# The opening of an attention and mixture-of-experts kernel: order of loads, roots, bias split and transposes

## The reference

```
xn = (x - mean(x)) / sqrt(var(x) + 1e-5)                # each row
q, k, v = xn @ wq.T + bq, xn @ wk.T + bk, xn @ wv.T + bv
off = 6 tanh(pw_w @ gelu(conv3(q) + dw_b) + pw_b)       # 16 heads x 12 samples a row
pos = clip(row + anchor + off, 0, 4095)                 # sampled by linear interpolation
attn = softmax(q . k[pos] / 4 - rel_scale |pos - row|)
s = (sum of attn * v[pos]) @ wo.T + bo
scores = xn @ Wr.T + br                                 # 8 experts; the best 2 of scores + biases_N
y = sum over these 2 of weight * ((silu(xn @ W1a + ..) * (xn @ W1b + ..)) @ W2 + bl2)
out = x + s * silu(y)
```

## Time and profile before

| | |
|---|---|
| runs | 1416.57, 1421.54, 1422.76 us |
| profiled execution | 1412.04 us, span from first to last instruction 1410.3 us |
| busy, share of the span | PE 94%, PEld 75%, DVE 88%, ACT 57%, POOL 53% |
| mean granted TensorE clock | 0.978 |
| DMA | 297.77 MB, mean 211 GB/s |

### The profile page before, as it was taken

How to read it: one execution, slowest core, us unless ns; L and a number is a source line. 1 busy time by engine, 2 the same in 40 slices (tenths; PEclk the granted TensorE clock), 3 DMA queues, 4 the chain that set the end, 5 groups by cost and what they waited for, 6 DMA issues and landing times. The chain is left out here.

```text
span 1410.3 us, 36326 instructions
## 1 busy us (share of the span) xinstructions
PE 1319.4 (94%) x13885; PEld 1057.6 (75%) x13885; DVE 1245.6 (88%) x1759; ACT 797.9 (57%) x1920; POOL 740.8 (53%) x441
## 2 busy tenths in 40 slices
PE   5998899897899999989999999999999978899987
PEld 4864566556788888868888888888888857777765
DVE  7856998987999999978999999999999999898971
ACT  2546788677545465435554454555465536676654
POOL 1000022101787887888886888886887862211031
PEclk9999999998999999999999999999999989999998
DMA  7952657856857777586777585877777469989679
GB/s 233 348 196 85 185 168 240 295 189 204 258 141 231 205 248 206 136 243 169 227 211 203 141 270 148 243 193 216 214 197 226 121 173 279 291 222 267 199 206 219
DMA packets 206905, 297.77 MB, mean 211 GB/s; under 512 B 21809, under 2 KB 164533, under 8 KB 206515
## 3 DMA queue, kind: packets, MB, share of 16 engines
q0 software_dynamic: 59968, 141.95, 38.3%
q1 hardware_dynamic: 119171, 141.43, 31.2%
q10 hardware_dynamic: 27632, 12.64, 3.5%
HBM read 186.30 MB, written 118.03 MB: 216 GB/s over the span
## 5 line engine op out<-in xcount | busy, mean ns | idle before, releaser
L1666 POOL DMA_INDIRECT moe_rows<-expert_mem,token_of x135 | 340.8, 2524 | 104.4 <-issue 69.7
L1633 POOL DMA_INDIRECT expert_mem<-xn_rows,token_of x131 | 250.0, 1908 | 54.4 <-issue 36.6
L1956 PE MATMUL pY<-expert_mem 128*128 x1080 | 253.2, 386 | 0.0
L1956 PEld LDWEIGHTS pY<-expert_mem 128*128 128x128 f32 x1080 | 199.0, 190 | 39.4 <-issue 13.6
L2154 DVE SCALAR_TENSOR_TENSOR mid<-pos_pair,mid 128x768 f32<-128x768 f32 x224 | 197.4, 952 | 0.5
L1800 ACT ACTIVATE expert_mem<-pA,b1sel 128x256 f32<-128x256 f32 (+1 forms) x300 | 110.1, 455 | 132.1 <-PE pA L1950 129.2
L1950 PE MATMUL pA<-mid,expert_mem 128*128 128x256 f32 (+1 forms) x816 | 171.0, 364 | 13.9 <-ACT mid L1772 6.8
L1950 PEld LDWEIGHTS pA<-mid,expert_mem 128*128 128x128 f32 x816 | 145.1, 194 | 33.8 <-issue 9.0
L262 DVE SCALAR_TENSOR_TENSOR mid<-mid 128x768 f32<-128x768 f32 x192 | 169.4, 951 | 0.0
L1950 PE MATMUL pB<-mid,expert_mem 128*128 128x256 f32 (+1 forms) x816 | 166.1, 357 | 0.0
L1811 ACT ACTIVATE expert_mem<-pB,b1sel 128x256 f32<-128x256 f32 (+1 forms) x300 | 110.7, 468 | 95.2 <-PE pB L1950 95.2
(11 more groups left out here) (282 smaller groups left out, 2409.0 us busy)
## 6 DMA issues: line engine op xcount, KB each, us to landing
expert_mem<-in_w_l POOLq DMA_DIRECT2D x51, 1024.0 KB, 7.7
bandT<-in_w_l POOLq DMA_DIRECT2D x24, 1024.0 KB, 7.5
band<-band_rows SPq DMA_DIRECT2D x256, 96.0 KB, 4.8
S_rows<-expert_mem SPq DMA_DIRECT2D x64, 376.0 KB, 4.0
band_rows<-wgt SPq DMA_DIRECT2D x12, 1536.0 KB, 9.2
pos_pair<-pos_rows SPq DMA_DIRECT2D x28, 384.0 KB, 5.8
xn_rows<-expert_mem SPq DMA_DIRECT2D x16, 512.0 KB, 5.4
v_rows<-expert_mem SPq DMA_DIRECT2D x16, 512.0 KB, 4.3
```

The source lines that it names most:

```text
L1633: nc.gpsimd.indirect_dma_start(out=xs[:, u, s], out_offset=None, in_=dram["xn"], in_offset=bass.IndirectOffsetOnAxis(ap=keep["inv"][:, 2 * ...
L1666: nc.gpsimd.indirect_dma_start(out=dram["moe"], out_offset=bass.IndirectOffsetOnAxis(ap=keep["inv"][:, 2 * n + s:2 * n + s + 1], axis=0), ...
L1956: mm = nc.tensor.matmul(pY[:, s], hid[:, h, c, s * P:(s + 1) * P], w2[:, c, ds(e * D, D)], start=False, stop=(closes and c == HC - 1))
```

## The change

On ScalarE the four small loads go; its order of roots and evacuations in the first steps is new. GpSimd issues the four small loads, behind its stores of zeros, counted on a semaphore of their own (`small_in`), which ScalarE and VectorE await behind the stage of rows. `wvr` gets its own semaphore too (`wvr_loaded`), awaited in front of values(0); TensorE's wait for the other weights goes in front of the projection. VectorE does its memsets first, then moments and normalise of steps 0, 1 and 2 in turn, then goes on as before, one step of moments ahead; the bias split goes behind the stage, in front of routing. TensorE transposes the identity 44 times into PSUM `pOff`, which isn't in use then, before transposes(0), and does values(0) before transposes(1).

```diff
--- before.py
+++ after.py
@@ -81,6 +81,7 @@
 PLACES_AT, EXPERTS_AT, MERGE_AT, TOKENS_AT = 7, 8, 13, 14
 OPEN_AT = 5
 ROWS_AHEAD = 4
+WAKE = 44
 BAND_SLOTS = 4
 MOE_SLOTS = 8
 W1_SLOTS = 3
@@ -403,6 +404,8 @@
         pRuns = pOff[:].rearrange("p u (b r) -> p u b r", r=P)
         pToken = pQK[:, 0, 0:HIGH]
 
+        wvr_loaded = sem("wvr_loaded")
+        small_in = sem("small_in")
         weights_in = sem("weights_in")
         bias_loaded = sem("bias_loaded")
         bias_zeroed = sem("bias_zeroed")
@@ -474,7 +477,7 @@
 
         TAIL = VROWS - TOKENS - REACH
         HALVES = SUBS // 2
-        WEIGHTS = 16 * 7
+        WEIGHTS = 16 * 2
         ROUTE_WEIGHTS = WEIGHTS + 16 * 5
         CONSTS = 8
 
@@ -633,6 +636,11 @@
             pool.dma_start(dram["xn"][TOKENS:, 0:D].rearrange("(s p) c -> p s c", p=P), zeros[:, None, :].broadcast_to([P, 2, D])).then_inc(pads_set, 16)
             pool.dma_start(dram["xn"][TOKENS:, D:].rearrange("(s p) c -> p s c", p=P),
                            zeros[:, None, 0:EXPERTS].broadcast_to([P, 2, EXPERTS])).then_inc(pads_set, 16)
+            pool.dma_start(keep["rel"][:], io["rel_scale"].partition_broadcast(P)).then_inc(small_in, 16)
+            pool.dma_start(keep["b1"][:], io["b_l1T"].rearrange("e p c -> p e c")).then_inc(small_in, 16)
+            pool.dma_start(br_bc[:], io["b_r"].partition_broadcast(P)).then_inc(small_in, 16)
+            pool.dma_start(bqk_col[:], io["b_qk"].rearrange("(k p) -> p k", p=P),
+                          allow_slow_non_contiguous=True).then_inc(small_in, 16)
             pool.wait_ge(gates_ready, 1)
             for q in range(4):
                 some = slice(q * TILES // 4, (q + 1) * TILES // 4)
@@ -676,14 +684,9 @@
 
         @block.scalar
         def _(act):
-            act.dma_start(wvr[:], io["w_vrT"].rearrange("(k p) n -> p k n", p=P)).then_inc(weights_in, 16)
+            act.dma_start(wvr[:], io["w_vrT"].rearrange("(k p) n -> p k n", p=P)).then_inc(wvr_loaded, 16)
             act.dma_start(wqk[:, :, 0:D], io["w_qkT"].rearrange("(k p) n -> p k n", p=P)[:, :, 0:D]).then_inc(weights_in, 16)
             act.dma_start(wqk[:, :, D:], io["w_qkT"].rearrange("(k p) n -> p k n", p=P)[:, :, D:]).then_inc(weights_in, 16)
-            act.dma_start(keep["rel"][:], io["rel_scale"].partition_broadcast(P)).then_inc(weights_in, 16)
-            act.dma_start(keep["b1"][:], io["b_l1T"].rearrange("e p c -> p e c")).then_inc(weights_in, 16)
-            act.dma_start(br_bc[:], io["b_r"].partition_broadcast(P)).then_inc(weights_in, 16)
-            act.dma_start(bqk_col[:], io["b_qk"].rearrange("(k p) -> p k", p=P),
-                          allow_slow_non_contiguous=True).then_inc(weights_in, 16)
 
             def root(n):
                 act.wait_ge(var_ready, n + 1)
@@ -780,7 +783,13 @@
             root(0)
             root(1)
             evacuate_x(0)
-            for n in range(STEPS):
+            root(2)
+            evacuate_v(0)
+            evacuate_x(1)
+            evacuate_x(2)
+            root(3)
+            evacuate_v(1)
+            for n in range(2, STEPS):
                 if n + 2 < STEPS:
                     root(n + 2)
                 if n + 1 < STEPS:
@@ -788,6 +797,7 @@
                 evacuate_v(n)
 
             act.wait_ge(weights_in, ROUTE_WEIGHTS)
+            act.wait_ge(small_in, 16 * 4)
             act.wait_ge(mask_set, 1)
             for m in range(2):
                 evacuate_k(m)
@@ -960,17 +970,21 @@
                 nc.tensor.matmul(pToken, pieces[0:LINEAR - P, 1, 0], goes_to[0:LINEAR - P, 1], start=False, stop=True).then_inc(token_done, 1)
 
             pe.wait_ge(zeros_set, 3)
+            for _ in range(WAKE):
+                nc.tensor.transpose(pOff[:, 0, 0:P], keep["ident"][:], keep["ident"][:])
             transposes(0)
-            pe.wait_ge(weights_in, WEIGHTS)
-            for n in range(STEPS):
+            pe.wait_ge(wvr_loaded, 16)
+            values(0)
+            transposes(1)
+            for n in range(1, STEPS):
                 if n + 1 < STEPS:
                     transposes(n + 1)
                 values(n)
 
+            pe.wait_ge(weights_in, ROUTE_WEIGHTS)
             for m in range(2):
                 project(m, 0)
                 project(m, 1)
-            pe.wait_ge(weights_in, ROUTE_WEIGHTS)
             for n in range(STEPS):
                 more = n + 2 < STEPS
                 head_scores(n, 0)
@@ -1307,7 +1321,6 @@
                     dve.sem_inc(keep["scored"], 1)
 
             V.memset(bias_in[:, D:], 0.0).then_inc(bias_zeroed, 1)
-            moments(0)
             for b in range(BATCH):
                 for col in (b * (SEQ + 2), b * (SEQ + 2) + SEQ + 1):
                     V.memset(qT[:, :, col:col + 1], 0.0)
@@ -1316,17 +1329,11 @@
             for x in range(SAMPLES):
                 V.memset(anchor[:, x], anchors()[sample_at(x)])
             V.memset(zero_te[:], 0.0)
-            moments(1)
-            normalise(0)
-            moments(2)
-            normalise(1)
-            dve.wait_ge(bias_loaded, 32)
-            parts = Chain(dve, bias_chain)
-            for k in range(NB):
-                parts(V.tensor_copy(bias_part[:, k], bias_in))
-                if k < NB - 1:
-                    parts(V.tensor_tensor(bias_in, bias_in, bias_part[:, k], ALU.subtract))
-            for n in range(2, STEPS):
+            for n in range(3):
+                moments(n)
+                normalise(n)
+            moments(3)
+            for n in range(3, STEPS):
                 if n + 1 < STEPS:
                     moments(n + 1)
                 normalise(n)
@@ -1352,10 +1359,17 @@
             chain(V.tensor_tensor(to_row[:, 0:1], to_row[:, 0:1], to_row[:, 1:2], ALU.add))
             chain(V.tensor_copy(base[:], base_i[:]))
             dve.wait_ge(weights_in, ROUTE_WEIGHTS)
+            dve.wait_ge(small_in, 16 * 4)
             V.tensor_scalar(keep["rel_low"][:], keep["rel"][:], 1.0 / SCALE, None, ALU.mult)
             V.tensor_scalar(keep["rel_fall"][:], keep["rel"][:], -2.0 / SCALE, None, ALU.mult)
             for b in range(BLOCKS):
                 V.memset(keep["shift"][:, b:b + 1], -float(b % WSUB))
+            dve.wait_ge(bias_loaded, 32)
+            parts = Chain(dve, bias_chain)
+            for k in range(NB):
+                parts(V.tensor_copy(bias_part[:, k], bias_in))
+                if k < NB - 1:
+                    parts(V.tensor_tensor(bias_in, bias_in, bias_part[:, k], ALU.subtract))
             shift_scores()
             slopes_of_k(0)
             slopes_of_k(1)
```

## The result

The changed kernel takes 1406.11 us (median of 9 runs, 1401.92 to 1410.5), the kernel before 1416.57 in the same sessions (9 runs, 1403.98 to 1422.76): a ratio of 0.993 with an interval of 0.9902 to 0.9959, so 10 us faster, 6 to 14. The prediction was 1416.4, range 1409 to 1422.5, for a gain of 5.1. It counted from 1421.54, the median of three runs; nine runs put the kernel before at 1416.57, so about half of the 10.3 between forecast and result is the base and the other half is gain that was not foreseen. The profiled execution took 1401.92 (span 1400.3) against 1412.04.

The account below looks back on a forecast made before the run. The stage of rows was taken to run at TensorE's pace with DMA close behind, its slow start never won back. Opening order 3.7 plus stall 1.4 gave 5.1 off 1421.54: 1416.4 us, range 1409 to 1422.5.

Parts of the forecast that it names:

- Milestones of the opening: Start of the rows' stage: normalised rows xn(n) and matmuls values(n) of 512-row step n come earlier, values(3) by 5.1 us.
- The stall of 1.4 for a store: Between values(2) and values(3): normalise(4) no longer waits for the store of xn(2), winning 1.4 us.
- The bias split: Five VectorE instructions, 2.77 us, leave the opening and hide in VectorE's wait of 8.61 behind the stage.
- The waits for the small loads: Before the projection: the four loads, now on GpSimd, land by 37 and are wanted after 80, costing nothing.
- a fast clock for values(0): Opening, TensorE: the first step's matmuls run at the fast clock because TensorE has just been busy; no delay.
- The rival on the clock: Opening, TensorE: the 44 transposes don't raise the clock; gain 4.0 or none, 1417.5 up to 1421.5 us; chance 0.18.
- The store's wait: Rows' stage: the 2.34 us wait for a store returns elsewhere, losing 1.4 to 2.3; about 1418.3 us; chance 0.18.
- stores that set the pace: Rows' stage: store landings above 7.4 us lengthen each step by half the excess; at 9, 1426 us; chance 0.05.
- What arrives at the end: Behind the rows' stage: time won at its last matmuls, values(15), moves all that follows; later stages bounded with 3 either way.
- a gain above 7: Whole kernel: more than 7 us won, by rows landing earlier or stalls that vanish too; chance 0.07.

Follow-up runs that it names:

- e7: Changed kernel with 58 instead of 44 identity transposes ahead of transposes(0) and 18 more between transposes(0) and values(0); 1402.94 us, ratio 0.9901.
- e4: Changed kernel with its first row loads held back by 20 added memsets on VectorE; 1437.59 us, ratio 1.0138.
- e6: Kernel before with only the four small loads moved to GpSimd and their waits ahead of the projection; 1409.12 us, ratio 0.9951.
- e9: Kernel before with two long VectorE additions per unit of the experts' stage cut into three and four pieces; 1410.0 us, ratio 0.994.
- e5: Changed kernel with three one-column copies, which nothing reads, added on ScalarE behind the stage of rows; 1407.0 us, ratio 0.9948.
- e8: Changed kernel with the four small loads back on ScalarE's queue; 1411.38 us, ratio 0.9978.
- e2: The changed kernel again, no edit; 1405.29 us, ratio 0.9913.

## Why the prediction was wrong

*Milestones of the opening.* xn(0) 10.78 (forecast 10.3), table load before 5, xn(3) 27.5 (25.8), values(2) 28.46 (26.9), values(3) 33.01 (31.5). The stall of 1.4 for a store is gone and stayed gone. The bias split costs nothing in its new place: VectorE still waits 6.03 behind it. The waits for the small loads show no idle time.

*Clock.* "I take no delay and a fast clock for values(0)" failed: 6.75 instead of 3.7. My reason was that TensorE had just been busy; it then stood still for 1.73 and 2.08. e7 sizes it at 0.7 to 1.4. The rival on the clock had the place right, and of its two reasons one: the gaps of 2 that stay between the groups are there. The other was that transposes don't raise the clock, and eight take 1.09 behind the 44, against 1.94 without them. The page "TensorE: Matmul & The Clock Gate", Part 4: PE-mode transpose, of the Trainium skill says that transposes don't count for the clock. This trace disagrees.

*The store's wait, stores that set the pace.* Neither came: three waits of 1.9 in all.

*What arrives at the end.* This is the step that failed. I wrote that time won at values(15) should move all that follows, and bounded later stages with 3 either way. The first half holds as far as e4 tells (0.95). The bound doesn't: the stretch between two table loads alone lost 11.75 and 4.09 in the two profiles of the kernel before and nothing in the changed one's. With the stage's 3.6 to 4.3 that makes 8 to 16, around the 10.5 and 12.3 that were timed. By its parts: the two kernels that win only the stretch (e6, e9) are timed at 0.995 and 0.994, some 7 to 8.5 less (intervals of about 4 either way); the two that win the stage and not all of the stretch (e5, e8) at 0.995 and 0.998. I gave 0.07 to a gain above 7, "by rows that land earlier or stalls that vanish too": its size came true by luck, through stalls 400 us behind the stage that I had not named.

The profile of before held the warning, in its waits from 563 to 634: TensorE waits 5.6 with "issue" as the only releaser, VectorE 8.4 for one evacuation, and GpSimd has issues of 6 to 7 where most take 2. I read the waits of the stage that the change touches, and none of those behind it.

*What is shown and what isn't.* Shown: the stretch has a floor at which TensorE never waits; the kernel before misses it by 4 or more in both its profiles; cutting VectorE's two additions reaches it with no change of the opening (e9). By one profile each: three idle instructions on ScalarE throw the changed kernel off it (e5), and the kernel before reaches it when its small loads leave ScalarE (e6). So the gain of the stretch is, by these profiles, not a merit of the new opening but a side effect of how it moved ScalarE's instructions. Not shown: where the 0.28 comes from, and how large the loss is on average in a kernel that misses the floor (2.7 to 11.75 in four profiles).

## What to carry to other kernels

Before you forecast that a late stage passes a shift on, look there for an engine that issues transfers and stands in long issues beside another engine's long instructions; its order can hang on tenths of a microsecond, and an edit far ahead can turn it. When a change gains more than its stage shows, measure between two marks that all kernels share, and repeat the kernel before: a stretch that agrees to 0.03 in ten profiles tells more than ten medians. Take the lever itself (here, shorter instructions on VectorE) and not the accident that moved it.

## What the runs showed of the hardware

GpSimd's indirect transfers are held by a long VectorE instruction that started before them: an issue of 6.29 ends 1.44 after the addition of 5.76 (528.51 to 534.27), one of 5.44 in e2 ends 1.45 after the same addition, and 2.24 is enough when it starts 0.83 ahead of it. In the profile of before all 23 indirect issues that start inside one of the two long additions end 0.8 to 1.5 behind its end, while the 13 that start up to 2 ahead of one and still run when it starts take 1.35 to 2.24. The Trainium skill has this in "SBUF — State Buffer", section "SBUF: two separate sides": a VectorE operation with two inputs in SBUF and a GpSimd operation that reads SBUF want the same pair of ports, whichever starts first keeps it for its whole instruction, and the other waits. The trace agrees on the order: behind the addition's start the scatter is held, ahead of it it gets away. That VectorE waits in its turn the trace doesn't show: the addition at 533.91 starts inside the scatter of 533.08 and takes the same 5.76.

The section "A bandwidth-pool intuition that's wrong (but worth ruling out)" of the same page of the Trainium skill lets the block of a held transfer last until 0.115 behind VectorE's instruction. The row has the end of the whole issue, 1.44 behind; how much of it is the issue's own work is not shown.

An unbroken run of short products can hold an issue as well: in e9 one at 557.47 lasts 6.69 beside products of 0.95 each, and ends 0.9 behind the last of them. Most are not held: of some 80 that start in or just ahead of such a run in e9, only the six named there last over 4.

TensorE's transposes alone raised its clock. In e7, with no matmul before them, 11 transposes are busy for the 2 us from 4 to 6, and 27 for the 2.7 us from 8.5 to 11.2, a step from the lower to the upper of the two levels. With no pause the clock then stayed: values(0) behind 84 transposes take 3.74, instead of the changed kernel's 6.75 behind a pause of 2.08. The column of granted clock prints 1.00 over all of e7's stage, the slow part too, so here the durations tell and not the column.
